# Second products of the last stage's sets: row groups of 32 in place of a block diagonal

## The reference, cut to what matters

```
perm     = (logits == max(logits, axis=token))          # one token per (group, e, s)
permuted = einsum('bntd,bntes->bnesd', grouped, perm)
inner    = relu(einsum('bnesd,esdf->bnesf', permuted, W1) + b1)     # f = 32
result_permuted = einsum('bnesf,esdf->bnesd', inner, W2) + b2       # d = 256
result   = einsum('bnesd,bntes->bntd', result_permuted, perm)
x = x + result
```

## Time and profile before

| | us |
|---|---|
| median of 3 runs | 830.35 (830.05 to 831.85) |
| profiled execution, its time | 839.29 |
| its span in the trace | 837.5 |
| mean granted TensorE clock in it | 0.949 of full speed |
| TensorE matmul busy | 728.9 (87%) |
| VectorE busy | 478.7 (57%) |
| ScalarE busy | 364.4 (44%) |
| GpSimd busy | 243.5 (29%) |

### The profile page before, as it was taken

How to read it: one execution, slowest core, us unless ns; L and a number is a source line. 1 busy time by engine, 2 the same in 40 slices (tenths; PEclk the granted TensorE clock), 3 DMA queues, 4 the chain that set the end, 5 groups by cost and what they waited for, 6 DMA issues and landing times.

```text
span 837.5 us, 16770 instructions
## 1 busy us (share of the span) xinstructions
PE 728.9 (87%) x6270; PEld 557.5 (67%) x6270; DVE 478.7 (57%) x1217; ACT 364.4 (44%) x672; POOL 243.5 (29%) x311
## 2 busy tenths in 40 slices
PE   7777988889898999888999999988778887888898
PEld 6554666556666665567988899976645555467775
DVE  4657676777788798471212122224658668563675
ACT  4355665456656646503232322202454454654213
POOL 6722434333444222122111211007244443421000
PEclk9988999999999999999999999998998899985999
DMA  9697766665754583439556666303584533070202
GB/s 190 100 220 112 110 84 91 91 92 92 97 82 77 86 179 129 153 125 363 188 157 202 185 197 177 140 24 100 77 125 68 89 60 58 16 321 4 102 13 89
DMA packets 60531, 101.85 MB, mean 122 GB/s; under 512 B 7278, under 2 KB 50734, under 8 KB 55440
## 3 DMA queue, kind: packets, MB, share of 16 engines
q1 hardware_dynamic: 58020, 95.29, 49.9%
q0 software_dynamic: 1872, 5.11, 2.9%
q10 hardware_dynamic: 560, 0.38, 0.1%
HBM read 55.22 MB, written 7.21 MB: 75 GB/s over the span
## 4 chain that ended last, share of the span: by engine, by line
PE 56%; DVE 17%; ACT 8%; issue 5%; DMA 4%; POOL 4%; another core or an unknown queue 3%; SPq 2%; ACTq 0%; POOLq 0%; DVEq 0%
PE MB L733 8%; PE PS L913 8%; PE U L924 8%; DVE nma L1295 5%; PE MB L840 5%; PE U L816 4%; PE MB L996 3%; PE MB L775 3%; PE MB L756 3%; PE PS L798 2%; PE MB L1006 2%; PE PS L970 2%; DMA mw<-in_mw 2%; DVE nmb L1295 2%
## 5 line engine op out<-in xcount | busy, mean ns | idle before, releaser
L1295 DVE TENSOR_REDUCE nma<-MB 128x2 f32<-128x512 f32 (+1 forms) x192 | 122.2, 671 | 39.9 <-PE MB L775 39.8
L1118 ACT ACTIVATE Pa<-PS 128x1024 f32<-128x1024 f32 (+1 forms) x96 | 97.8, 1025 | 33.4 <-PE PS L798 32.0
L924 PE MATMUL U<-mw,mdT 128*128 x368 | 85.3, 386 | 4.9 <-DVE mdT L1487 2.3
L913 PE MATMUL PS<-mzT,mw 128*128 128x128 f32 x736 | 86.3, 275 | 3.5 <-DMA mw<-in_mw 3.5
L775 PE MATMUL MB<-QKa 99*128 99x120 bf16 (+1 forms) x512 | 70.8, 250 | 18.8 <-DVE nma L1295 4.9
L913 PEld LDWEIGHTS PS<-mzT,mw 128*128 128x128 f32 x736 | 84.1, 192 | 4.4 <-DMA mw<-in_mw 4.3
L1495 DVE TENSOR_TENSOR yt<-U,mb 128x256 f32<-128x256 f32 x23 | 9.8, 424 | 131.8 <-PE U L924 131.8
L924 PEld LDWEIGHTS U<-mw,mdT 128*128 128x128 f32 x368 | 69.3, 193 | 14.7 <-issue 5.9
L775 PEld LDWEIGHTS MB<-QKa 99*128 99x128 bf16 x512 | 37.7, 99 | 50.0 <-DVE nma L1295 13.4
L1586 POOL TENSOR_TENSOR mv<-mv,vec 128x2 f32<-128x2 f32 (+1 forms) x40 | 30.5, 764 | 115.6 <-DVE mv L1252 63.9
L798 PE MATMUL PS<-QKa 101*128 101x256 bf16 (+1 forms) x384 | 59.5, 279 | 1.8 <-DMA QKa<-mTa 1.8
(11 more groups left out here) (220 smaller groups left out, 1393.4 us busy)
## 6 DMA issues: line engine op xcount, KB each, us to landing
mw<-in_mw SPq DMA_DIRECT2D x31, 1024.0 KB, 6.2
QKa<-spa SPq DMA_DIRECT2D x144, 128.0 KB, 4.6
Qb<-spb SPq DMA_DIRECT2D x48, 128.0 KB, 4.2
Oa<-Uba SPq DMA_DIRECT2D x16, 256.0 KB, 2.6
v<-in_v SPq DMA_DIRECT2D x1, 4096.0 KB, 13.3
v<-in_v SPq DMA_DIRECT2D x4, 1024.0 KB, 12.0
yb<-yt SPq DMA_DIRECT2D x23, 128.0 KB, 1.7
QKa<-spa SPq DMA_DIRECT2D x24, 120.0 KB, 4.0
```

What stands on the lines that cost most here:

```text
L913: i = e.matmul(ps[:, 128 * f:128 * f + 128], w[:, k, 128 * f:128 * f + 128], zz[:, k, :], start=k == 0, stop=k == 1)
L924: i = e.matmul(U[:, 0:256], mdT[j % 2][:, f, :], w2[:, bass.ds(expert[j], 1), f, :], start=f == 0, stop=f == 7)
L1118: e.activation(p[0:keys, :], ps[0:keys, :], ACT.Exp, scale=0.25).then_inc(sems["exp"], 1)
L1295: e.tensor_reduce(A.nm[qt][:, h0:h0 + heads], b[:, 0:heads * keys].rearrange("p (h s) -> p h s", h=heads), AX.X, ALU.max, negate=True).the ...
```

## The change

The block diagonal goes. A step "e2" is now a group g of 16 pairs (8 steps in place of 32). Each pair is a product with 32 rows: the weights are 32 partitions of v2 by 128 columns, and the moving operand is 32 partitions of Tmp[b] by 64 columns. The row group j writes a bank of its own; the groups use the four banks of PS0 and PS1 (even g) and U, MB0, MB1, MB2 (odd g) in turn. The relu is done in place in Tmp[b] by one instruction of 128 partitions. Of a group's four banks VectorE takes out two or three as before, with the bias. ScalarE copies the others to R (j = 3 always, j = 2 in groups 1, 3, 4 and 6), and GpSimd adds the bias to these in SBUF. The clearing of BD goes, and the loads of v2 for batches 1 and 2 no longer wait for the four "e1". The two semaphores of the constants become one.

```diff
+def down_on(g, j):
+    return "a" if j == 3 or j == 2 and g in (1, 3, 4, 6) else "b"
-    out += [("e2", b, q) for b in range(4) for q in range(8)]
+    out += [("e2", g) for g in range(8)]
+    def set_bank(g, j):
+        return ((U, MB[0], MB[1], MB[2])[j][:, :] if g % 2 else PS[j // 2][:, 512 * (j % 2):512 * (j % 2) + 512])
+    def set_rows(g, j):
+        first = 16 * g + j
+        return (R[:, :, :, first:16 * g + 16:4], c2[:, :, first:16 * g + 16:4])
 TensorE
-            g.wait_ge("relu", b + 1)
-            g.free(BANKS.free["e2", b, q])
-            for k in range(2):
-                i = e.matmul(m[:, 256 * k:256 * k + 256], v2[:, 8 * b + q, 128 * k:128 * k + 128], bd[:, q, :, :],
-                             start=True, stop=True)
-            i.then_inc(sems["e2"], 1)
+            b, half = n // 2, n % 2
+            g.wait_ge("relu", b + 1)
+            if n == 0:
+                g.wait_ge("sorted_a", copies("a", 7, 1))
+                g.wait_ge("sorted_b", copies("b", 7, 1))
+            elif n == 1:
+                g.wait_ge("up", 4)
+                g.wait_ge("u_copied", 48)
+            else:
+                g.wait_ge("down", downs("b", n - 2))
+                g.wait_ge("down_a", downs("a", n - 2))
+            for q in range(4):
+                for k in range(2):
+                    for j in range(4):
+                        i = e.matmul(banks[j][:, 128 * q + 64 * k:128 * q + 64 * k + 64],
+                                     v2[32 * j:32 * j + 32, 4 * n + q, 128 * k:128 * k + 128],
+                                     Tmp[b][32 * j:32 * j + 32, 4 * half + q, :], start=True, stop=True)
+                        if (q, k) == (3, 1):
+                            i.then_inc(sems["e2"], 1)
 first transpose
-            g.wait_ge("down", 32)
+            g.wait_ge("down", downs("b", 7))
+            g.wait_ge("biased", downs("a", 7))
 ScalarE
-            for j in range(4):
-                i = e.activation(BD[b % 2][32 * j:32 * j + 32, :, j, :], Tmp[b][32 * j:32 * j + 32, :, :], ACT.Relu)
-            i.then_inc(sems["relu"], 1)
+            e.activation(Tmp[b][:, :, :], Tmp[b][:, :, :], ACT.Relu).then_inc(sems["relu"], 1)
+        def sets_down(n):        # the banks of "a"
+                    e.activation(dst, set_bank(n, j).rearrange("p (s k n) -> p k n s", s=4, k=2), ACT.Identity
+                                 ).then_inc(sems["down_a"], 1)
 VectorE, the banks of "b"
+                    e.tensor_tensor(dst, set_bank(n, j).rearrange("p (s k n) -> p k n s", s=4, k=2), over(bias, 64, 2),
+                                    ALU.add).then_inc(sems["down"], 1)
 GpSimd
-            for b in BD:
-                e.memset(b[:, :, :, :], 0.0).then_inc(sems["bd0"], 1)
+        def sets_down(n):        # the banks of "a", after ScalarE's copy
+                    e.tensor_tensor(dst, dst, over(bias, 64, 2), ALU.add).then_inc(sems["biased"], 1)
 SyncE, ahead of the loads of v2 for batches 1 and 2
-            g.wait_ge("e1", 4)
```

More of the change, by code:

```diff
@@ L190, in copy_on, with downs @@
     return "a" if c == 0 or b < 2 else "b"
+def down_on(g, j):
+    return "a" if j == 3 or j == 2 and g in (1, 3, 4, 6) else "b"
+def downs(engine, g):
+    return sum(down_on(i, j) == engine for i in range(g + 1) for j in range(4))
 def order():
@@ L604, in build @@
     z01 = at("z01", [128, NT, 2, 256], BF, y_at)
-    BD = [at(f"BD{i}", [128, 8, 4, 64], F32, y_at + 8192 * i) for i in range(2)]
     c2 = ta.new("c2", [128, 2, 128])
@@ L614, in build @@
              "z_turned split_f max_turned exp u_copied g_turned zt_done mid_a f_turned perm0 perm_turned sorted_a "
-             "relu zeros turned_a split_h mhalf ohb0 rs split_r split_l bias xy fr fl bd0 "
+             "relu consts turned_a split_h ohb0 rs split_r split_l bias xy fr fl down_a biased "
              "z_t proj v_t mx mt sc pv p1 p2 gt logits gr marks slot_mm slots table ztr up_mm down_mm ft choice pt gp e1 e2 turn comb "
@@ L988, in sets_up @@
             i.then_inc(sems["e1"], 1)
-        def sets_down(b, q):
-            m, bd = bank("e2", b, q), BD[b % 2]
+        def sets_down(n):
+            b, half = n // 2, n % 2
+            banks = [set_bank(n, j) for j in range(4)]
             g.wait_ge(f"d_v2{(0, 1, 2, 0)[b]}", 32 if b in (0, 3) else 16)
             g.wait_ge("relu", b + 1)
-            g.free(BANKS.free["e2", b, q])
-            for k in range(2):
-                i = e.matmul(m[:, 256 * k:256 * k + 256], v2[:, 8 * b + q, 128 * k:128 * k + 128], bd[:, q, :, :],
-                             start=True, stop=True)
-            i.then_inc(sems["e2"], 1)
+            if n == 0:
[15 more added lines that the diff above has]
+                            i.then_inc(sems["e2"], 1)
         def turn(m):
             b = bank("tu", m)
-            g.wait_ge("down", 32)
+            g.wait_ge("down", downs("b", 7))
+            g.wait_ge("biased", downs("a", 7))
             g.free(BANKS.free["tu", m])
@@ L1199, in scalar @@
                 "sc": scores, "pv": values, "gt": gate_turn, "ro": tile_in, "be": tile_turn, "in": first_loads,
-                "ft": front_turn, "fw": front_choice, "fp": perm_turn, "gc": sort, "e1": sets_up, "tu": turn}
+                "ft": front_turn, "fw": front_choice, "fp": perm_turn, "gc": sort, "e1": sets_up, "e2": sets_down, "tu": turn}
         for what, *key in STEPS:
@@ L1531, in sets_up, with sets_down @@
                             over(vec[:, V_BM1 + 8 * b:V_BM1 + 8 * b + 8], 64, 2), ALU.add).then_inc(sems["up"], 1)
-        def sets_down(b, q):
-            s = 4 * (8 * b + q)
-            g.wait_ge("d_c2", 16)
-            g.wait_ge("e1", 4)
-            g.wait_ge("e2", 8 * b + q + 1)
-            e.tensor_tensor(R[:, :, :, s:s + 4], bank("e2", b, q)[:, :].rearrange("p (k s n) -> p k n s", k=2, s=4),
-                            over(c2[:, :, s:s + 4], 64, 2), ALU.add).then_inc(sems["down"], 1)
+        def sets_down(n):
+            for j in range(4):
+                if down_on(n, j) == "b":
+                    dst, bias = set_rows(n, j)
+                    g.wait_ge("d_c2", 16)
+                    g.wait_ge("e1", 4)
+                    g.wait_ge("e2", 4 * n + j + 1)
+                    e.tensor_tensor(dst, set_bank(n, j).rearrange("p (s k n) -> p k n s", s=4, k=2), over(bias, 64, 2),
+                                    ALU.add).then_inc(sems["down"], 1)
         def turn(m):
@@ L1654, in front_choice, with sets_down @@
             e.tensor_tensor(z2[:, two(b), :], Yz[n % 2][:, :, :], z01[:, two(b), 1, :], ALU.subtract).then_inc(sems["fl"], 1)
-        def clear():
-            g.wait_ge("sorted_a", copies("a", 7, 1))
-            g.wait_ge("sorted_b", copies("b", 7, 1))
-            for b in BD:
-                e.memset(b[:, :, :, :], 0.0).then_inc(sems["bd0"], 1)
+        def sets_down(n):
+            for j in range(4):
+                if down_on(n, j) == "a":
+                    dst, bias = set_rows(n, j)
+                    g.wait_ge("d_c2", 16)
+                    g.wait_ge("down_a", downs("a", n) - (down_on(n, 3) == "a" and j == 2))
+                    e.tensor_tensor(dst, dst, over(bias, 64, 2), ALU.add).then_inc(sems["biased"], 1)
         does = {"in": constants, "on": rows_of_ones, "na": norm_stats, "qp": lambda n: split_rest("qp", n),
```

21 lines of the change are left out of this document (10 added, 11 removed).

## The result

The changed kernel takes 840.25 us, median of 20 runs (834.97 to 846.12). The kernel before, run beside it, takes 834.71 us, median of 20 (828.42 to 842.24; the 830.35 of the front are the median of its first three). The ratio is 1.0067, interval [1.0042, 1.0092]: about 5.6 us slower. 820.0 was forecast, 816 to 825.5.

The account below looks back on a forecast made before the run. TensorE was taken to bound the second products, 28.6 us to the first transpose. The new stage at 17.8 us gives -10.8, early loads +0.4: -10.4 from 830.35, said as 820.0 us, range 816 to 825.5.

Parts of the forecast that it names:

- part 2: Second products, emptying 32 banks on VectorE, ScalarE and GpSimd: with waits the stage takes 17.8 us, 10.8 less than 28.6.
- Part 1: Second products, TensorE's work: 512 records at 27 ns, weight loads four side by side, 13.7 us or 1.71 per group.
- A: Second products: weight loads not hidden behind their own row group's matmul, stage 22.7 us, kernel 824.9; chance 0.09.
- C: Second products: float32 loads into different row groups don't overlap fully, kernel 831.9 (two at a time) or 859; chance 0.10.
- Rule and row: Trainium skill: weight loads overlap a running matmul only in another row group; trace row: 107 ns loads hidden on same rows.
- rival D: Instruction fetch beside v2 loads stalls TensorE 3 us or more, or GpSimd's strided addition takes 1.6: 823 to 824; chance 0.09.
- rival B: Second products: clock falls 3.5 us in, stage 26.2 us, transposes give back 2.5: 830.4, no change; chance 0.06.
- Part 3: Waits moved around the second products: v2 loads issued earlier, beside the first products, cost 0.4 us; other moves nothing.
- What would show it: List of signs in the new profile, such as 512 records in 14.5 to 16 us and first transpose near 798.

Follow-up runs that it names:

- contig: Changed kernel with pairs dealt out so each bank's results are runs of four neighbours in R: 828.55 us, ratio 0.9922 to the kernel before.
- contig_warm: Changed kernel with writes in runs of four, plus 12 never-read matmuls ahead of the first transpose: 824.89 us, ratio 0.9861 to the kernel before.
- contig_split: Changed kernel with writes in runs of four and batch 2's v2 load put behind the first products: 837.36 us, median of six; ratio 0.9883 from two.
- v2_late: Changed kernel with the wait for the four first products put back ahead of the v2 loads for batches 1 and 2: 838.37 us, one run.
- changed_fill: Changed kernel plus never-read matmuls, 8 ahead of each of groups 2 to 7 and 24 before the first transpose: 840.09 us, ratio 1.0066.

## Why the prediction was wrong

The step that failed is **part 2**, the prices of the engines that empty the banks: GpSimd's addition was priced at 1.16 us and took 2.08, VectorE's instruction at 0.69 (0.61 back to back) and took 1.14, ScalarE's at 0.62 and took 1.13.

- **Part 1, right.** Row groups do load side by side: 64 records in 2.02 us at full clock, 1.71 and latency forecast, so rivals A and C fall, and with C the only slower case that I had. Rule and row disagreed on overlap, and the row was the better guide.
- **Part 2, wrong, 10.9 us.** I kept 0.61 for VectorE and 0.62 for ScalarE though the destination had changed from runs of four to every fourth element. I saw the step only for GpSimd, and bounded it at 1.6 where it took 2.08 (rival D). With the forecast prices the forecast stage comes out: contig, 18.1 us. No row of before shows such a write, so this price had to be bounded from both sides for all three engines. At the measured prices the schedule of part 2 gives the long stage: GpSimd can start at 779.2 and works for 24.2 us, so 803.4; with 1.0 us of waiting for ScalarE it ended at 804.4.
- **The clock, 2.7 us behind the stage.** I gave its fall 0.06 (rival B), 3.5 us into the stage, because the products use the rows in part. It came 7.3 us in, after TensorE had waited 1.3 us for banks where part 2 had 0.55. The same products with short waits kept 1.00 in contig_warm. But in contig_split it fell before TensorE had waited for any bank, so the longer wait is a suspect and not a shown cause. B's price behind the stage was about right: 2.5 for the transposes at half clock, 2.7 measured. Its stage of 26.2 was too short for the changed kernel, since it kept the prices of part 2. (Its sum leaves out the 0.4 of part 3: 830.35 - 2.4 + 2.5 + 0.4 is 830.8, not 830.4.)
- **Part 3, wrong in size, 2.0 us.** I named the fetch of instructions beside the v2 loads and took 0.4 of "nothing to 2.3"; the stage grew by 2.4, and its gaps by 3.4. I reasoned that the transfers would be nearly over. But they started at 760, with the first products, and TensorE stood still from 764.55 on, in the middle of them.
- **The start of the sum** was off too. 820.0 is 10.4 under 830.35, the median of three runs; twenty runs gave 834.71. The 8.9 us by which I took a run with profile to be longer "throughout" were spread: the changed kernel's profiled run, 838.05, lies under its median. The ratio is free of this: -10.4 us forecast, +5.6 measured.
- **What would show it** was of use: "VectorE's 20 instructions at 0.69" and "the gap longer than 1.19" were the two lines that failed, and both named their cause.

What stays open. Why the clock is at half from the start of the second products in some runs. In both kernels where it was seen a 1 MB load ran beside (266 GB/s in contig_split). But there the clock fell at 775.7, a little before the load's bytes began to move at 776.0, and v2_late had 282 GB/s beside from 776 on and kept 1.00 until 781.7, so the load is not shown to be the cause. What makes the clock fall in the changed kernel is open in the same way. And it is open how much of the 2 us of the first products reaches the end.

## What to carry to other kernels

When a result is laid out anew, look at the innermost run of each operand in SBUF before you price its instruction: an operation with the same shape and engine cost 1.3 to 2 times as much here when each element of the write stood alone, and a permutation of the weights gave the runs back for nothing. When work moves off the engine that bounds, the engines behind it and that engine's clock can become the bound together; test them apart, and also both at once, since removing either alone may show nothing. A load moved to run beside short matmuls may lengthen their gaps, as it did here.

## What the runs showed of the hardware that I had not expected

- Writing 128 x 512 float32 with each element alone: VectorE 0.68 to 1.03 (other engines at rest) or 1.14 us, ScalarE 0.60 to 1.13, GpSimd (which also reads so) 1.04 to 2.08 at 16 bytes and to 1.40 at 512.
- Float32 weight loads of 32 rows in four row groups overlap almost fully at full clock: 28.6 ns per load of 128 columns ((2.02 - 0.22) / 63, where 0.22 is the latency of a record), close to a quarter of the 107 ns estimated for one alone.
- After the wait for the last banks TensorE worked at half clock for another 5.9 us (804.5 to 810.4, changed kernel) and 5.5 us (800.2 to 805.7, contig). In contig, twelve matmuls that nobody reads took that away; in the changed kernel, where the wait was longer, 24 did not (changed_fill).
- With a load of 2 MB beside it, at up to 421 GB/s, the first gap of the first products was 3.18 us long, where it is 1.19 us without.
